# Third and fourth tile's first norm formed feature-major on GpSimd, from a second input layout, with scales broadcast through DRAM

## The reference

```python
def _layernorm(x, axis=-1, eps=1e-05):
    m = jnp.mean(x, axis=axis, keepdims=True)
    v = jnp.var(x, axis=axis, keepdims=True)
    return (x - m) / jnp.sqrt(v + eps)

# attention part, on n = _layernorm(x)
q = silu(n @ Wq1 @ Wq2)
f = sigmoid(n @ Wk1 @ Wk2)
v = n @ Wv
a = exp(log_sigmoid(f))
k = 1.0 - a
h = scan(h = a * h + k * v)            # along the 512 tokens
out = q * h
out = out * rsqrt(mean(out * out) + 1e-6) * norm_w
x = x + _layernorm(out @ Wo)

# feed-forward part, on x' = _layernorm(x): six blocks
x' = gelu(x' @ W1[i].T + B1[i]) @ W2[i].T + B2[i] + x'
x' = layernorm with gain and bias      # after blocks 0 to 4
x = x + _layernorm(x')
```

## Time and profile before

| | |
|---|---|
| median of 3 runs | 625.76 us (625.5 to 625.86) |
| the profiled execution | 625.7 us |
| its span, first to last instruction | 623.7 us |
| TensorE busy | 617.8 us (99%) |
| VectorE, ScalarE, GpSimd busy | 466.2, 408.0, 249.6 us |
| mean granted clock of TensorE | 0.998 of full speed |

### The profile page before, as it was taken

How to read it: one execution, slowest core, us unless ns; L and a number is a source line. 1 busy time by engine, 2 the same in 40 slices (tenths; PEclk the granted TensorE clock), 3 DMA queues, 4 the chain that set the end, 5 groups by cost and what they waited for, 6 DMA issues and landing times.

```text
span 623.7 us, 8865 instructions
## 1 busy us (share of the span) xinstructions
PE 617.8 (99%) x2893; PEld 516.4 (83%) x2893; DVE 466.2 (75%) x826; ACT 408.0 (65%) x690; POOL 249.6 (40%) x231
## 2 busy tenths in 40 slices
...
DMA packets 56301, 25.13 MB, mean 40 GB/s; under 512 B 46784, under 2 KB 52288, under 8 KB 56256
## 3 DMA queue, kind: packets, MB, share of 16 engines
...
q10 hardware_dynamic: 2400, 0.52, 0.4%
...
## 4 chain that ended last, share of the span: by engine, by line
PE 96%; DVE 1%; ACT 1%; DMA 0%; POOL 0%; issue 0%; POOLq 0%; DVEq 0%; ACTq 0%
PE BK L166 47%; PE BK L356 40%; PE BK L306 4%; PE BK L371 1%; PE BK L267 1%; PE BK L270 1%; PE BK L268 1%; PE BK L240 1%; DVE ST L677 0%; PE BK L260 0%; PE BK L251 0%; PE BK L252 0%; DMA X<-in_x 0%; PE BK L230 0%; DVE R L706 0%
## 5 line engine op out<-in xcount | busy, mean ns | idle before, releaser
L973 ACT ACTIVATE HH<-BK,SM 128x512 fp32r<-128x512 f32 x192 | 131.8, 688 | 134.9 <-PE BK L166 128.8
L569 DVE TENSOR_TENSOR HL<-BK,HH 128x512 fp32r<-128x512 f32 x192 | 130.7, 684 | 62.7 <-ACT BK L979 60.2
L166 PE MATMUL BK<-XH,WL 128*128 128x512 f32 x416 | 162.4, 390 | 0.0
L166 PE MATMUL BK<-XL,WH 128*128 128x512 f32 x416 | 162.1, 390 | 0.0
L166 PE MATMUL BK<-XH,WH 128*128 128x512 f32 x416 | 162.0, 389 | 0.0
L356 PE MATMUL BK<-HH,WL 128*128 128x512 f32 x368 | 143.6, 390 | 0.0
L356 PE MATMUL BK<-HL,WH 128*128 128x512 f32 x368 | 143.2, 389 | 0.0
L356 PE MATMUL BK<-HH,WH 128*128 128x512 f32 x368 | 143.2, 389 | 0.0
L979 ACT ACTIVATE BK<-BK,SM 128x512 f32<-128x512 f32 x192 | 125.4, 656 | 1.6 <-issue 1.6
L166 PEld LDWEIGHTS BK<-XH,WL 128*128 128x128 f32 x416 | 78.1, 188 | 16.6 <-DVE MS L551 0.3
L166 PEld LDWEIGHTS BK<-XH,WH 128*128 128x128 f32 x416 | 78.1, 188 | 16.4
...
## 6 DMA issues: line engine op xcount, KB each, us to landing
STG<-in_w SPq DMA_DIRECT2D x24, 512.0 KB, 3.8
G<-sums SPq DMA_DIRECT2D x160, 8.0 KB, 1.7
...
X<-in_x SPq DMA_DIRECT2D x3, 512.0 KB, 8.0
R<-turns SPq DMA_DIRECT2D x3, 512.0 KB, 4.0
turns<-SA SPq DMA_DIRECT2D x12, 64.0 KB, 2.0
sums<-P SPq DMA_DIRECT2D x40, 8.0 KB, 1.4
R<-in_wv SPq DMA_DIRECT2D x1, 512.0 KB, 5.8
```

Source lines behind the costliest of these rows:

```text
L166: r = eng.matmul(dst, s, m, start=i == 0, stop=i == len(todo) - 1)
L569: eng.tensor_tensor(HL[:, g % HR, :], bank["mm1", n, j][:, :], HH[:, g % HR, :].bitcast(f32), ALU.subtract).then_inc(S["hlo"], 1)
L973: eng.activation(HH[:, g % HR, :], bank["mm1", n, j][:, :], ACT.Gelu, bias=B1[:, 8 * (n // 4) + j:8 * (n // 4) + j + 1]).then_inc(S["ghi"], 1)
```

## The change

For tiles 2 and 3 the token-major result and its transposes go. The host gives the kernel the input of those tiles a second time, feature-major (`xt`). `ldxt(t)` loads it into `R[:, t]`. Once the scales and offsets of the tile's tokens are there, `row_out(t)` writes the 8 values of each partition to DRAM, as two rows of 512, and `row_in(t)` reads the two rows back into all 128 partitions of MB. GpSimd then multiplies and adds in place (`l1_mul`, `l1_add`, for each half k), and `xhi1` and `xlo1` read SBUF and not PSUM. The statistics stay as they were. The two matrices of scales RS and NBS become two parts of one tensor SC. The memsets `half` and `quarter` stand ahead of `idle_in`. All lists up to the regular part, and the lists of the end, are in a new order; what they hold is otherwise the same.

```diff
-def sandwich(nc, x, wq1, wk1, wq2, wk2, wv, wo, small, w1, w2, ident_in, out):
+def sandwich(nc, x, xt, wq1, wk1, wq2, wk2, wv, wo, small, w1, w2, ident_in, out):
...
-        RS = sb("RS", [128, NT, 4])
-        NBS = sb("NBS", [128, NT, 4])
+        SC = sb("SC", [128, NT, 2, 4])
+        RS, NBS = SC[:, :, 0, :], SC[:, :, 1, :]
...
+        ROWS = nc.dram_tensor("rows", (2, 2, TOK), f32, kind="Internal").ap()
...
+        def turned(t, k):
+            return R[:, t, 2 * k:2 * k + 2, :].rearrange("p c f -> p (c f)")
...
             def turn1(t, k, b):
                 claim(b)
-                pe.wait_ge(S["l1_nm"], 4 * t)
+                pe.wait_ge(S["l1_nm"], 4)
...  (TensorE's list, first part)
-            spin(); first_turn0(7); first_turn1(5, 4); first_hh(0, 0, 2); first_hh(1, 0, 0); first_lh(0, 0)
-            first_hl(0, 0); first_hh(0, 1, 7); first_lh(1, 0); first_hl(1, 0); first_lh(0, 1); first_hl(0, 1)
-            first_hh(1, 1, 3); first_lh(1, 1); first_hl(1, 1); zq(0, 0, 5); zq(0, 1, 4); zk(0, 0, 2); zk(0, 1, 0)
-            zq(0, 2, 1); v(0, 0, 2); v(0, 1, 3); zk(0, 2, 5); zk(0, 3, 0); v(0, 2, 1); zq(0, 3, 5); v(0, 3, 2)
-            proj(0, 0); turn1(1, 0, 0); turn1(1, 1, 3); proj(0, 1); up(1, 0, 4); u(1, 0); up(1, 1, 3); u(1, 1)
-            proj(0, 2); zq(1, 0, 5); zq(1, 1, 0); zq(1, 2, 1); zk(1, 0, 4); v(1, 0, 2); zq(1, 3, 0); proj(0, 3)
-            zk(1, 1, 3); v(1, 1, 4); rms(0, 2); zk(1, 2, 1); turn1(2, 0, 5); turn1(2, 1, 0); v(1, 2, 3); v(1, 3, 2)
-            zk(1, 3, 1); up(2, 0, 4); u(2, 0); up(2, 1, 0); u(2, 1); proj(1, 0); proj(1, 1); zq(2, 0, 1); zq(2, 1, 3)
-            zk(2, 0, 4); v(2, 0, 5); proj(1, 2); zq(2, 2, 0); zk(2, 1, 2); turn3(0, 0, 1); turn3(0, 1, 3); proj(1, 3)
-            v(2, 1, 4); mm1(0, 0, 1); mm1(0, 1, 2); rms(1, 3); mm1(0, 2, 0); zq(2, 3, 3); mm1(0, 3, 1); mm1(0, 4, 2)
-            zk(2, 2, 0); mm2(0, 0); mm2(0, 1); mm1(0, 5, 1); proj(2, 0); v(2, 2, 0); mm2(0, 2); proj(2, 1)
-            turn3(1, 0, 3); turn3(1, 1, 2); mm2(0, 3); mm1(0, 6, 1); turn1(3, 0, 2); turn1(3, 1, 3); mm2(0, 4)
-            up(3, 0, 2); u(3, 0); mm1(0, 7, 3); zk(2, 3, 1); mm2(0, 5); up(3, 1, 0); u(3, 1); zq(3, 0, 1); v(2, 3, 3)
+            spin(); first_turn0(7); first_turn1(5, 4); first_hh(1, 0, 0); first_hh(0, 0, 3); first_lh(0, 0)
+            first_hl(0, 0); first_lh(1, 0); first_hl(1, 0); first_hh(0, 1, 5); first_lh(0, 1); first_hl(0, 1)
+            first_hh(1, 1, 6); first_lh(1, 1); first_hl(1, 1); zq(0, 0, 3); zq(0, 1, 5); zq(0, 2, 4); zk(0, 0, 0)
+            zk(0, 1, 3); v(0, 0, 2); zk(0, 2, 5); v(0, 1, 0); zk(0, 3, 4); v(0, 2, 5); zq(0, 3, 3); v(0, 3, 2)
+            proj(0, 0); turn1(1, 0, 0); turn1(1, 1, 4); proj(0, 1); up(1, 0, 1); u(1, 0); up(1, 1, 0); u(1, 1)
+            v(1, 0, 4); zq(1, 0, 5); zq(1, 1, 1); zk(1, 0, 3); zk(1, 1, 2); zq(1, 2, 5); proj(0, 2); proj(0, 3)
+            v(1, 1, 1); zq(1, 3, 3); zk(1, 2, 5); rms(0, 4); zk(1, 3, 0); v(1, 2, 2); v(1, 3, 3); up(2, 0, 1)
+            up(2, 1, 4); u(2, 0); u(2, 1); v(2, 0, 5); proj(1, 0); zq(2, 0, 0); zq(2, 1, 1); proj(1, 1); zk(2, 0, 2)
+            proj(1, 2); turn3(0, 0, 2); zq(2, 2, 0); turn3(0, 1, 4); proj(1, 3); zk(2, 1, 1); mm1(0, 0, 2); v(2, 1, 4)
+            rms(1, 3); mm1(0, 1, 1); zq(2, 3, 3); mm1(0, 2, 0); zk(2, 2, 5); mm1(0, 3, 1); mm1(0, 4, 2); mm2(0, 0)
+            mm1(0, 5, 0); mm2(0, 1); proj(2, 0); mm2(0, 2); mm2(0, 3); v(2, 2, 0); turn3(1, 0, 1); mm1(0, 6, 2)
+            mm1(0, 7, 3); mm2(0, 4); turn3(1, 1, 1); up(3, 0, 2); u(3, 0); zk(2, 3, 0); up(3, 1, 3); u(3, 1)
...  (VectorE)
             def xlo1(t, k):
                 ve.wait_ge(S["xhi1"], 2 * t + k + 3)
+                if t > 1:
+                    eng.tensor_tensor(XL[:, L1_SLOT[t], k, :], turned(t, k), XH[:, L1_SLOT[t], k, :].bitcast(f32),
+                                      ALU.subtract).then_inc(S["xlo1"], 1)
+                    return
...  (VectorE's list, from q(0, 0) on)
-            first_ulo(1, 1); q(0, 0); l1_st(1, 0); l1_st(1, 1); l1_mv(1, 0); l1_st(1, 2); l1_mv(1, 1); q(0, 1)
-            l1_mv(1, 2); l1_st(1, 3); q(0, 2); l1_mv(1, 3); kv(0, 0); l1_st(2, 0); scan(0, 0); kv(0, 1); o(0, 0)
-            scan(0, 1); l1_mv(2, 0); kv(0, 2); olo(0, 0); o(0, 1); scan(0, 2); olo(0, 1); q(0, 3); o(0, 2); one()
-            xlo1(1, 0); xlo1(1, 1); kv(0, 3); olo(0, 2); scan(0, 3); ulo(1, 0); l1_st(2, 1); o(0, 3); l1_mv(2, 1)
-            l1_st(2, 2); ulo(1, 1); l1_mv(2, 2); l1_st(2, 3); q(1, 0); l1_mv(2, 3); q(1, 1); olo(0, 3); q(1, 2)
+            first_ulo(1, 1); q(0, 0); l1_st(1, 0); one(); l1_st(1, 1); l1_st(1, 2); l1_mv(1, 0); l1_mv(1, 1); q(0, 1)
+            l1_st(1, 3); q(0, 2); l1_mv(1, 2); l1_mv(1, 3); kv(0, 0); l1_st(2, 0); scan(0, 0); kv(0, 1); o(0, 0)
+            scan(0, 1); kv(0, 2); olo(0, 0); o(0, 1); scan(0, 2); olo(0, 1); o(0, 2); l1_st(2, 1); xlo1(1, 0)
+            xlo1(1, 1); l1_mv(2, 0); l1_st(2, 2); l1_st(2, 3); l1_mv(2, 1); l1_mv(2, 2); l1_mv(2, 3); kv(0, 3)
...  (later in it: olo(1, 0); xlo1(2, 0); xlo1(2, 1); olo(1, 1))
...  (ScalarE)
             def xhi1(t, k):
+                if t > 1:
+                    ac.wait_ge(S["l1_add"], 2 * t + k - 3)
+                    if t == 3:
+                        ac.wait_ge(S["v"], 8)
+                    eng.activation(XH[:, L1_SLOT[t], k, :], turned(t, k), ACT.Copy).then_inc(S["xhi1"], 1)
+                    return
...  (ScalarE's list around tile 2, new)
+            xhi1(1, 0); xhi1(1, 1); a(0, 3); osq(0, 0); tq(0, 3); uhi(1, 0); osq(0, 1); osq(0, 2); uhi(1, 1)
+            ohi(0, 2); tq(1, 0); tq(1, 1); ohi(0, 3); wp_hi(2); t1(1, 0); a(1, 0); tq(1, 2); osq(0, 3); t1(1, 1)
+            wp_hi(3); a(1, 1); ohi(1, 0); tq(1, 3); t1(1, 2); a(1, 2); osq(1, 0); t1(1, 3); ohi(1, 1); xhi1(2, 0)
+            a(1, 3); xhi1(2, 1); wp_hi(4); l2_nm(0, 0); l2_nm(0, 1); l2_nm(0, 2); l2_nm(0, 3); uhi(2, 0); osq(1, 1)
+            uhi(2, 1); gelu_in(); ohi(1, 2); tq(2, 0); tq(2, 1); l3_nm(0, 0); l3_nm(0, 1); l3_nm(0, 2); l3_nm(0, 3)
...  (GpSimd)
+            def l1_mul(t, k):
+                po.wait_ge(S[f"xt{t}"], 16)
+                po.wait_ge(S["row_in"], 16 * (t - 1))
+                eng.tensor_tensor(turned(t, k), turned(t, k), MB[:, 0, :], ALU.mult).then_inc(S["l1_mul"], 1)
+
+            def l1_add(t, k):
+                po.wait_ge(S["l1_mul"], 2 * t + k - 3)
+                eng.tensor_tensor(turned(t, k), turned(t, k), MB[:, 1, :], ALU.add).then_inc(S["l1_add"], 1)
...  (GpSimd's list, new)
+            mhalf(); half(); quarter(); idle_in(); f_rs(0); f_rs(1); wq1_lo(); wk1_lo(); wq2_lo(); wk2_lo()
+            nw_minus(); wv_lo(); wo_scaled(); l1_ve(1); bias(); l1_rs(1); l1_ng(1); l1_nb(1); wo_lo(); wp_lo(1, 0)
+            wp_lo(1, 1); l1_ng(2); l1_ve(2); l1_rs(2); l1_nb(2); ssum(0, 1); ssum(0, 2); wp_lo(2, 0); wp_lo(2, 1)
+            ssum(0, 3); l1_mul(2, 0); l1_mul(2, 1); l1_add(2, 0); l1_add(2, 1); l2_ng(0); l2_ve(0); l2_rs(0); l2_nb(0)
+            x1(0, 0); x1(0, 1); x1(0, 2); x1(0, 3); l3_ve(0); l3_ng(0); l3_rs(0); l3_nb(0); wp_lo(3, 0); ssum(1, 1)
+            ssum(1, 2); wp_lo(3, 1); ssum(1, 3); l1_ng(3); l1_ve(3); l1_rs(3); l2_ng(1); l2_ve(1); l2_rs(1); l1_nb(3)
+            l2_nb(1); wp_lo(4, 0); x1(1, 0); wp_lo(4, 1); x1(1, 1); x1(1, 2); x1(1, 3); l1_mul(3, 0); l3_ve(1)
+            l3_ng(1); l3_rs(1); l3_nb(1); l1_mul(3, 1); l1_add(3, 0); l1_add(3, 1); ssum(2, 1); ssum(2, 2); ssum(2, 3)
...  (SP)
+            def ldxt(t):
+                if t == 2:
+                    sp.wait_ge(S["wk2_lo"], 1)
...
+                eng.dma_start(R[:, t, :, :].rearrange("p c f -> p (c f)"), xt[t - 2]).then_inc(S[f"xt{t}"], 16)
+
+            def row_out(t):
+                sp.wait_ge(S["l1_nb"], t)
+                eng.dma_start(ROWS[t - 2].rearrange("w (c p) -> p w c", c=4), SC[:, t, :, :],
+                              allow_slow_non_contiguous=True).then_inc(S["row_out"], 16)
+
+            def row_in(t):
+                sp.wait_ge(S["row_out"], 16 * (t - 1))
+                if t == 3:
+                    sp.wait_ge(S["l1_add"], 2)
+                eng.dma_start(MB[:, :, :], ROWS[t - 2].unsqueeze(0).to_broadcast([128, 2, TOK])).then_inc(S["row_in"], 16)
...
-            for p in range(1, 5):
-                ldp(p)
-            put1(0)
-            got1(0)
-            put2(0)
-            ldp(5)
-            got2(0)
-            ldp(6)
-            ldp(7)
+            ldp(1); ldp(2); ldp(3); ldxt(2); row_out(2); row_in(2); ldp(4); ldxt(3); row_out(3); row_in(3); ldp(6)
+            put1(0); ldp(5); got1(0); put2(0); got2(0); ldp(7)
```

250 lines of the change are left out of this document (121 added, 129 removed).

## The result

The changed kernel takes 641.73 us in the median of five runs (640.42 to 642.36), the kernel before in the same five rounds 625.82: a ratio of 1.0252, with an interval of 1.0241 to 1.0263. The forecast was 624.2, and the range to 626.4 did not hold it. The profiled execution is the 640.42 one, 14.72 us above the profiled one of before.

The account below looks back on a forecast made before the run. TensorE was taken as the bound, 96% of the chain and without gaps from 12 to 600 us. Removed transposes give 1.74 us, less a 0.2 us wait, 1.5 gained from 625.76: forecast 624.2, range 623.6 to 626.4.

Parts of the forecast that it names:

- step 3: Tile 2's row_out, 1,024 pieces of 4 bytes: lands after 2.8 us, bounded by 1.4 below and 6.6 above.
- The prediction's own sign of being wrong: row_out taking over 5 us, or gaps ahead of proj, turn3(0, 0) or mm2(0, 0).
- The rule weighed there: row_out: if read-modify-write made 4-byte writes cost twice the small-piece rate, landing and forecast about 1.6 us worse.
- Step 4: Tile 2's row_out queued behind two 512 KB loads: queue clear at about 32.3, landing between 32.4 and 34.3.
- step 1: Tile 2's first-norm statistics on VectorE: the last l1_mv(2) comes at 27.8 in the new order.
- The one collision of 0.6 us: VectorE's olo(1, 0), at about 40.4, locks out GpSimd's chain of four: 0.6 us, so TensorE waits 0.2.
- always costs VectorE or GpSimd something: Shared port pair: by the lock rule, more GpSimd work always costs one of the two engines; without it, 1.74.
- Rival B: up(2, 0): scales late, TensorE waits 3.4 us, time 627.4; decisive if row_in(2) lands after 40.2; chance 0.15.
- slack 4 us even with 4 us more for row_out: Tile 3 at up(3, 0), due at 83.4, its four operations ending near 78: claimed slack 4 us.
- what is queued behind: Instructions behind the late ones on GpSimd, ScalarE and SP: turn3(0, 0) slack 0.8; only put1(0) behind row_in(3).
- Rival A: After 44 us, VectorE and the shared lock take the gain back: waits 1.0 to 1.3, time 625.1, chance 0.29.
- VectorE lost no work: VectorE, 0.9 us free in 29, keeps its work while TensorE comes 0.87 us earlier to everything behind 44.

Follow-up runs that it names:

- experiment 2: Kernel before plus seven unused DMAs on SP of differing piece size and spacing: 1,024 adjacent 4-byte pieces 10.0 us, 128 bytes apart 2.9; kernel 625.73 us.
- experiment 7: Kernel before plus seven other unused stores: 1,024 4-byte pieces every 8 bytes 4.3 us, every 64 bytes 2.4, adjacent 8.7; no kernel time given.
- experiment 9: Changed kernel with each token's scale and offset side by side, so row_out writes 512 pieces of 8 bytes: 625.98 us, ratio 1.0002 to the kernel before.
- experiment 1: Changed kernel with scales transposed on VectorE and row_out writing 32 pieces of 128 bytes in four DMAs: 625.30 us, ratio 0.9992 to the kernel before.
- experiment 13: experiment 1 with tile 1's q, kv and o on VectorE done on one column in place of 512: 624.49 us, ratio 0.9974 to the kernel before.
- experiment 10: experiment 5 with all statistics of tile 0's second norm moved ahead of kv(1,1), scan(1,1) and o(1,1) on VectorE: 625.68 us, ratio 1.0000.
- experiment 12: experiment 10 with GpSimd's multiplications and additions on one column in place of 512: 625.64 us, ratio 0.9999 to the kernel before.
- experiment 14: Kernel before with tile 1's q, kv and o on one column in place of 512, partner of experiment 13: 626.17 us, ratio 1.0000.
- experiment 6: experiment 1 with the change's eight GpSimd multiplications and additions on one column in place of 512: 625.13 us, ratio 0.9992 to the kernel before.
- experiment 5: experiment 1 with ulo(2,0), uhi(2,0), xhi1(2,0) and q(1,3) further ahead in the written order: 625.08 us, ratio 0.9990 to the kernel before.

## Why the prediction was wrong

**The step that failed is step 3**, "I take 2.8, since pieces of 64 and 128 bytes are nearest", with 6.6 as the bound from above. Measured: 10.5 and 10.6 us. The prediction's own sign of being wrong, row_out over 5 us, came true. The bound was drawn from rows of 64 bytes and more; in none of them do two pieces share 8 bytes, and experiments 2, 7 and 9 show that most of the price comes where they do. The pieces that are nearest in size were not nearest in kind: 1,024 pieces of 64 bytes land in 2.2 us. The form of the term was wrong too, a price for each piece on a DMA engine: the packets of tile 3's store are through 1.6 us after its issue, and the other 9.1 us come behind the last of them.

The rule weighed there, of the Trainium skill ("DMA: Bandwidth & Descriptors", section "Specifications": under 512 bytes the DMA reads, modifies and writes), pointed the right way but was given 1.6 us. Beside it stand the numbers here: all the probe's pieces are under 512 bytes, and they take from 2.2 to 10.0 us for the same count, so the rule by size alone does not give the time. Read-modify-writes of one word that must follow one another would fit these numbers; no run shows the mechanism itself.

**Step 4, the queue, was not the cause.** Tile 3's `row_out` has nothing ahead and takes 10.64 us, tile 2's 10.46. In tile 2 the queue is clear and the store's last packets are through by 32.6 us, near the 32.3 of step 4; it lands at 39.75 all the same. With the 8-byte pairs the queue does show, 5.3 against 3.7 us.

**The other steps held.** Statistics done at 27.3 (step 1: 27.8), `l1_nb(2)` at 29.3 (29.6), `row_in` 4.1 us (4.0), GpSimd free at 37.7 (38.1), four operations in 4.9 us (5.1 less overlap), `up(2, 0)` due at 44.2: experiment 1, in which the scales are in time, has it at 44.30. The one collision of 0.6 us fell elsewhere, on the second norm's small operations: in experiment 1 GpSimd has, under an `olo` and an `xlo1` of VectorE,

```profile
43.61 0.61 POOL L1194 TENSOR_SCALAR NM<-MV 128x4 f32<-128x4 f32 x1 [0.66 <-DVE MV L479]
44.18 0.65 POOL L1229 TENSOR_TENSOR VE<-MV,MS 128x4 f32<-128x4 f32 x1
44.90 1.34 POOL L1237 TENSOR_TENSOR SC<-VE,MH 128x4 f32<-128x4 f32 x1
```

0.61, 0.65 and 1.34 us for operations of 0.20, 0.20 and 1.02. That agrees with the lock of the Trainium skill's "SBUF — State Buffer", section "SBUF: two separate sides", and VectorE's two are operations on two SBUF tensors. At the end it was worth little or nothing: experiment 13 has the same collisions (0.61, 0.64 and 1.40 us) and keeps almost the whole gain, and experiments 10 and 12, where these operations take 0.20 and 1.02 again, are no faster, though in another order. The sentence that more GpSimd work "always costs VectorE or GpSimd something" goes further than the rule, which is about an overlap with such an operation.

**Rival B is what happened, at another price.** Place and mechanism are its: TensorE waits at `up(2, 0)` for scales that land after 40.2 (they landed at 43.9). It was given 3.4 us by the bound of step 3. It lacked two terms. One is the clock: a wait of 5.5 us brought 2.7 us of matmuls at 1.2 GHz behind it, which a sum of waits doesn't hold. The other is tile 3, "slack 4 us even with 4 us more for row_out": with 7.8 us more, on a walk that the first wait had shifted, it broke. That slack did not follow from its own numbers either: with the four operations ending near 78 and `up(3, 0)` at 83.4 it is some 5 us, and 4 us more for row_out leave about 1. And it broke at a place that was not examined, the third norm of tile 1 behind `l1_mul(3, 0)`. The list "what is queued behind" was made for `row_in(2)`, and names of `row_in(3)` only one DMA behind it.

**Rival A is half right.** Once the scales are in time the kernel stands at 625.1 to 626.1, where A said 625.1. Its first half, VectorE full while TensorE comes earlier, is borne out by experiments 13 and 14, with the reservation made there. Its second, GpSimd's added work and the lock, is refuted by 6 and 12 for the long operations, and 13 speaks against it for the small ones. So with row_out at the forecast's own 2.8 us the likeliest time would still have been A's: experiment 1, whose scales are in time, took 625.30 and not 624.2. The forecast allowed waits at `up(2, 0)` only, and took "VectorE lost no work" as harmless. In a stretch where VectorE has 0.9 of 29 us free, 0.87 us less for TensorE came out in full in none of the orders tried.

What stays open: what happens between a store's last packet and its landing when 4-byte pieces touch (8-byte pieces that touch do not show it), whether it matters that neighbours come from different partitions, as they do in every one of these stores, and whether some order of VectorE's instructions would get the rest. Three orders were tried, and none got under 625.08. The best of them, experiment 5, is 0.1% faster than the kernel before by its interval, less than counts as a difference here.
